# A four-layer graph network in one kernel: when the target rows are turned and exchanged in its first stage, and the order of two products in its second

## The chip, the cores and the metric

The kernel runs on one core of a Trainium2 chip. The metric is the time of one execution on the device, in microseconds (us); lower is better. TensorE is written PE in the rows (PEld: its weight loads), VectorE DVE, ScalarE ACT, GpSimd POOL, and SP is the engine that does nothing here but issue transfers.

## The reference

Four graph layers run one after the other on a table of 100,000 nodes with 128 features each, and 50,000 edges (`src`, `dst`, sorted by `dst`). After each layer the result is added to its input and each row is normalized. Layers 0 and 1 are those of this change:

```python
def _L0_gnn_ref(x, W, b, src, dst):
    diff = x[dst] - x[src]
    max_diff = jax.ops.segment_max(diff, dst, num_segments=x.shape[0])
    max_diff = jnp.where(jnp.isneginf(max_diff), 0, max_diff)
    return jax.nn.relu(jnp.concatenate([x, max_diff], axis=1) @ W + b)

def _L1_gnn_ref(x, feature1, feature2, edge_index, batch, ...):
    src, dst = (edge_index[0], edge_index[1])
    x = _swish(x @ lin_W.T + lin_b)
    f1 = feature1 @ f1_W1.T @ f1_W2.T
    f2 = feature2 @ f2_W1.T @ f2_W2.T
    agg1 = jax.ops.segment_sum(f1 * x[src], dst, num_segments=n)
    h1 = agg1 @ conv1_rel_W.T + conv1_rel_b + x @ conv1_root_W.T
    h1 = _swish(h1 @ lin1_W.T + lin1_b)
    agg2 = jax.ops.segment_sum(f2 * x[src], dst, num_segments=n)
    h2 = ...                                   # as h1, with the second set of weights
    h = jnp.concatenate([h1, h2], axis=1) @ cat_W.T + cat_b
    h = h + x
    for i in range(3):
        h = _swish(h @ lins_W[i].T + lins_b[i]) + h
    ...                                        # graph norm over all nodes, final product

x = _layernorm(x + _L0_gnn_ref(x, L0_gnn_W, L0_gnn_b, src, dst))
x = _layernorm(x + _L1_gnn_ref(x, edge_attr_54, edge_attr_18, edge_index, batch0, ...))
...                                            # layers 2 and 3 in the same manner
```

## The kernel before

Nodes and edges are cut into blocks of 512 rows (4 tiles of 128): 196 node blocks (`NB`) and 98 edge blocks (`EB`). The program is a row of stages with a barrier between them. The change touches two of them:

- **nodes01** computes, for every node block, layer 0 without edges and the part of layer 1 that needs none, and for every edge block the rows of those nodes that have incoming edges in layer 0. Each engine has a hand-written order of work in `step(t)`, one step for each node block, with an edge block in every second step. So an even step and the odd step behind it make a **pair**: two node blocks and one edge block. Engines meet only at semaphores (`wait_ge`).
- **edges1** does layer 1 once more for the nodes that have edges, one edge block a step, with the two segment sums as scans.

In nodes01 an edge block goes this way. POOL gathers the target rows into `p_xd` (L729). DVE turns them in squares of 32 by 32 into `p_xdt` (`turn_squares`, L138). SP exchanges the groups of 32 partitions with four transfers into `p_xdT` (`swap_groups`, L156). PE multiplies them: L817, in the odd step, then L818 for the running minimum `p_run` of the scan (L986). DVE adds and normalizes (L967, L993, L212, L1002), POOL raises to the power -1/2 (L761), DVE makes the shift `p_nm` (L957) and ACT applies both (L227). Node blocks go through the same statistics, and then through h1, h2 (L797, L800, L860, L862), their concatenation (L826, L827, then L973 on DVE) and three residual layers: products L784, L806 and L832 on PE, activations L848 on ACT, additions L903 on DVE. The rest is turned and exchanged in the same way for `p_xT` (input rows) and `p_x1T` (normalized rows); all three exchanges are issued by SP in one hand-written order, behind waits:

```python
for t in range(0, NB + 12, 2):          # SP, nodes01: one turn for each pair
    ...                                 # p_xT, load of x, store of p_o, store of p_oe
    ...                                 # hT, p_x1T, p_xdT, t1T, pen
```

In edges1 the steps of PE end with the concatenation (L1264, L1265), the third residual product (L1270) and the product of the block's own rows (L1275), whose activation `q_xx` (L1334) is what L1228 of the next step multiplies. The residual products are L1222, L1242 and L1270, with L1293 on ACT and L1355 on DVE behind each; L1422 on DVE is behind L1265; L1432 and L1437 are the two scans.

Of the kernel before, what the change touches and what calls it, by code (L numbers as in the profile page):

```python
# [13 lines left out]
G = 4  # L14
# [546 lines left out]
def nodes01(nc, a, tab, s, first, arrivals, ring, to_edges1, NB, EB):  # L561


    with ExitStack() as ctx:
# [65 lines left out]
        def _(sp):  # L630
# [3 lines left out]
            for t in range(0, NB + 12, 2):  # L634
# [16 lines left out]
                if live(e, EB):  # L651
                    sp.wait_ge(e_applied, e + 1)
                    sp.dma_start(e_v[e], oe[:, e % 2]).then_inc(e_saved[e % 2], DMA)
                n = t - 12
# [10 lines left out]
                e = t // 2 - 1 - BEHIND  # L665
                if live(e, EB):
                    sp.wait_ge(xd_squared, e + 1)
                    after(sp, e_product, e - 1)
                    swap_groups(sp, xdT[:, e % 2].rearrange("p j a i -> p a j i"), xd_turned[:, :, :], xdT_in[e % 2])
# [225 lines left out]
        def _(dve):  # L895
# [17 lines left out]
            def step(t):  # L913
# [45 lines left out]
                if even and e.live(EB):  # L959
                    dve.wait_ge(xd_in[e.of(2)], landed(2, e, G))  # L960
                    if e.past(1):
                        dve.wait_ge(xdT_in[e.back(1).of(2)], landed(2, e.back(1), 4))
                    turn_squares(nc, xd_turned[:, :, :].rearrange("p c (j i) -> p c j i", j=G), xd[:, e.of(2)]).then_inc(xd_squared, 1)
# [34 lines left out]
                if not even and q.live(QB):  # L998
                    lo, hi = batch(q)
                    dve.wait_ge(counted, counted_by(q))  # L1000
                    after(dve, rooted, q.b - 1)
                    nc.vector.tensor_scalar(guard[:, q.of(2), lo:hi], st[:, q.of(2), lo:hi, SQUARES], 1.0 / H, LN_EPS,  # L1002
                                            ALU.mult, ALU.add).then_inc(guarded, 1)
            n_chain = [0]
# [58 lines left out]
def edges1(nc, a, tab, s, ring, to_edges1, h_saved, NB, EB, LAST):  # L1063


    with ExitStack() as ctx:
# [148 lines left out]
        def _(pe):  # L1215
            def step(t):
# [43 lines left out]
                if n.live(EB):  # L1260
                    pe.wait_ge(h1_ready, n.b + 1)
                    pe.wait_ge(h2_ready, n.b + 1)
                    after(pe, r0_ready, n.b)
                    nc.tensor.matmul(flat(bank_h), s["cat"][:, 0, :], h1[:, n.of(2), :], start=True, stop=False)  # L1264
                    nc.tensor.matmul(flat(bank_h), s["cat"][:, 1, :], h2[:, n.of(2), :],  # L1265
                                     start=False, stop=True).then_inc(cat_done, 1)
                n = t.back(2)
# [4 lines left out]
                if t.live(EB):  # L1272
                    pe.wait_ge(own_in[t.of(4)], landed(4, t, 4))
                    pe.wait_ge(active_g, t.b + 1)
                    nc.tensor.matmul(flat(bank_l), s["lin"][:, :], by_row(flat(own[:, t.of(4)])),  # L1275
                                     start=True, stop=True).then_inc(lined_o, 1)
# [12 lines left out]
        def _(act):  # L1289
# [10 lines left out]
            def step(t):  # L1300
# [27 lines left out]
                n = t.back(2)  # L1328
                if n.live(EB):
                    residual(2, n)  # L1330
                if t.live(EB):
                    act.wait_ge(lined_o, t.b + 1)
                    after(act, r0_ready, t.b - 1)
                    nc.scalar.activation(xx[:, t.of(2), :], flat(bank_l), ACT.Silu, bias=col(LIN_B)).then_inc(active_o, 1)  # L1334
                if t.fixed and t.b == MASK_AT:
                    act.wait_ge(turned, 1)
                    nc.scalar.activation(mask16[:, 0:4, :], bank_t[0:MC, 0:4, :], ACT.Copy).then_inc(copied, 1)
                    act.wait_ge(turned, 2)
                    nc.scalar.activation(mask16[:, 4:7, :], bank_t[0:MC, 0:3, :], ACT.Copy).then_inc(copied, 1)
# [959 lines left out]
```

## Time and profile before

| | |
|---|---|
| median of 3 runs | 5377.8 us (5353.22, 5377.8, 5377.81) |
| profiled execution, its own time | 5359.57 us |
| its span, first to last instruction | 5357.8 us |
| PE busy | 4172.5 us, 78% of the span |
| DVE busy | 4291.2 us, 80% |
| ACT busy | 3570.0 us, 67% |
| POOL busy | 4022.1 us, 75% |
| nodes01, its first and last turn of target rows | 67.0 and 1857.6 us |
| edges1, roughly | from 1900 to 3000 us |

Busy is the time in which an engine executes something; the rest of the span it waits. PE's ends of matmuls are modelled, so that a matmul of 512 columns reads as 1.02 us for its two passes although the next begins 0.86 us after it did. For the order of events on PE, read starts.

### The profile page before, as it was taken

The page shows a single profiled execution, that of the slowest core. Times are in us where ns is not written, and L with a number is a line of the kernel's source. Part 1 is how long each engine was busy: PE and PEld are TensorE (multiplying, and loading weights), DVE is VectorE, ACT ScalarE, POOL GpSimd, SP SyncE. Part 2 cuts the span into 40 slices and gives each one's busy share as a digit, 9 for nine tenths or more (in the row PEclk, how much of TensorE's full clock was granted, in tenths as well). Part 3 has the DMA queues.
Part 4 walks back from the last instruction along what each step waited for, and adds up shares of the span by engine and source line. Part 5 has one row for each costly group of instructions (what it writes and reads, how often), then busy time and mean ns, then how long its engine had stood idle before and what let it go on. Part 6 is the DMA issues. An engine that isn't in the chain of part 4 may idle for free. (4 is left out here: it accounts for less than half of the span.)

```text
span 5357.8 us, 82513 instructions
## 1 busy us (share of the span) xinstructions
PE 4172.5 (78%) x18043; PEld 2613.2 (49%) x18166; DVE 4291.2 (80%) x8844; ACT 3570.0 (67%) x9029; POOL 4022.1 (75%) x4129
## 2 busy tenths in 40 slices
PE   6899999999999969999999888888577745550000
PEld 3455555555555534444444588878454535540000
DVE  7789888889999748887888799999788844457776
ACT  3667766667777636666666688888688844446665
POOL 6677877778787777777777277777777767777777
PEclk9999999999999989999999999999655557665555
DMA  7888998999999748777777699999799867774443
GB/s 191 199 217 224 220 226 218 219 218 230 226 229 225 182 107 244 204 205 206 208 204 207 227 380 375 376 375 379 262 284 282 278 202 229 230 238 151 136 135 102
DMA packets 1057580, 1239.08 MB, mean 231 GB/s; under 512 B 554591, under 2 KB 724121, under 8 KB 1057335
## 3 DMA queue, kind: packets, MB, share of 16 engines
q1 hardware_dynamic: 951542, 1085.52, 65.5%
q0 software_dynamic: 100352, 149.23, 13.1%
q10 hardware_dynamic: 5440, 1.80, 0.1%
q14 instruction: 182, 1.48, 0.1%
q8 instruction: 64, 1.05, 0.1%
HBM read 648.66 MB, written 438.76 MB: 203 GB/s over the span
## 5 line engine op out<-in xcount | busy, mean ns | idle before, releaser
L848 ACT ACTIVATE p_s<-p_ps,cols 128x512 f32<-128x512 f32 x588 | 402.2, 684 | 192.6 <-PE p_ps L832 119.6
L1199 POOL DMA_INDIRECT ring_rows<-t_rows,home_cols x384 | 419.1, 1091 | 118.9 <-issue 88.3
L198 POOL DMA_INDIRECT out<-u_res,scatter_cols x392 | 406.9, 1038 | 121.8 <-issue 118.1
L191 POOL DMA_INDIRECT u_rows<-t_rows,home_cols x392 | 387.5, 988 | 145.6 <-issue 118.6
L191 POOL DMA_INDIRECT ring_rows<-t_rows,home_cols x400 | 394.7, 987 | 129.6 <-issue 114.3
L736 POOL DMA_INDIRECT home<-edge_row_cols,scatter_cols x392 | 401.8, 1025 | 119.2 <-issue 119.2
L729 POOL DMA_INDIRECT p_xs<-in_x,src_cols x388 | 393.3, 1014 | 123.0 <-issue 114.0
L729 POOL DMA_INDIRECT p_xd<-in_x,dst_cols x388 | 384.6, 991 | 106.8 <-issue 95.7
L1208 POOL DMA_INDIRECT home_cols<-home,src_cols x376 | 378.0, 1005 | 111.4 <-issue 86.0
L227 ACT ACTIVATE p_o<-p_v,p_nm,p_rs 128x128 f32<-128x128 f32 x784 | 321.5, 482 | 138.6 <-DVE p_nm L957 137.6
L212 DVE BATCH_NORM_STATS2 r_counts<-r_v 128x6 f32<-128x256 f32 x980 | 373.2, 422 | 10.6 <-issue 0.5
L227 ACT ACTIVATE r_x<-r_v,r_nm,r_rs 128x128 f32<-128x128 f32 x784 | 321.7, 482 | 82.3 <-DVE r_nm L1779 82.3
L1832 ACT ACTIVATE u_o<-u_x,cols,u_rs 128x128 f32<-128x128 f32 x392 | 161.0, 482 | 286.9 <-DVE u_x L1821 286.9
L1293 ACT ACTIVATE q_s<-q_ps,cols 128x512 f32<-128x512 f32 x294 | 202.0, 687 | 184.6 <-PE q_ps L1270 131.0
L1612 PEld LDWEIGHTS r_ps_n<-r_wn,r_h 128*128 128x128 f32 x2352 | 313.4, 194 | 10.5 <-issue 0.3
L1612 PE MATMUL r_ps_n<-r_wn,r_h 128*128 128x128 f32 x2352 | 313.5, 277 | 5.4 <-issue 0.3
L1590 POOL TENSOR_TENSOR r_v<-r_x,default_row 128x512 f32<-128x512 f32 x192 | 244.3, 1273 | 71.8 <-ACT r_x L227 71.8
L761 POOL TENSOR_TENSOR p_rs<-p_guard,minus_half 128x12 f32<-128x12 f32 (+2 forms) x101 | 236.7, 2344 | 76.7 <-DVE p_guard L1002 76.0
L234 PE MATMUL u_ps_s<-ident,u_weighted 128*128 128x128 f32 x392 | 104.4, 420 | 227.9 <-DVE u_weighted L2190 227.7
L903 DVE TENSOR_TENSOR p_r<-p_s,p_r 128x512 f32<-128x512 f32 x392 | 261.3, 667 | 19.2 <-ACT p_s L848 19.1
L791 PEld LDWEIGHTS p_ps<-w_swapped,p_xT 128*128 128x128 f32 x1568 | 221.2, 202 | 113.1 <-issue 102.3
L860 ACT ACTIVATE p_h<-p_ps,cols 128x512 f32<-128x512 f32 x196 | 134.7, 687 | 211.7 <-PE p_ps L797 211.7
(305 smaller groups left out, 13770.7 us busy)
## 6 DMA issues: line engine op xcount, KB each, us to landing
ring_rows<-in_x SPq DMA_DIRECT2D x98, 512.0 KB, 6.5
p_xT<-p_xt SPq DMA_DIRECT2D x392, 128.0 KB
t_rows<-p_o SPq DMA_DIRECT2D x98, 512.0 KB
p_x1T<-p_oT SPq DMA_DIRECT2D x392, 128.0 KB
hT<-ring_own SPq DMA_DIRECT2D x98, 512.0 KB
q_hn<-hT SPq DMA_DIRECT2D x98, 512.0 KB, 4.7
r_h<-hT SPq DMA_DIRECT2D x98, 512.0 KB
r_x<-t_rows SPq DMA_DIRECT2D x98, 512.0 KB
```

Of the source, the lines that this page charges most:

```text
L191: nc.gpsimd.indirect_dma_start(out=rows[:, j, :], out_offset=None, in_=table, in_offset=bass.IndirectOffsetOnAxis(ap=idx[:, j:j + 1], axis ...
L198: nc.gpsimd.indirect_dma_start(out=table, out_offset=bass.IndirectOffsetOnAxis(ap=idx[:, j:j + 1], axis=0), in_=rows[:, j, :], in_offset=N ...
L212: i = nc.vector.bn_stats(st[:, j:j + 2, :].rearrange("p j k -> p (j k)"), v[:, j:j + 2, :].rearrange("p j f -> p f j"))
L227: i = nc.scalar.activation(dst[:, j, :], v[:, j, :], ACT.Identity, bias=nm[:, j:j + 1], scale=rs[:, j:j + 1])
L729: nc.gpsimd.indirect_dma_start(out=rows[:, j, :], out_offset=None, in_=a["x"], in_offset=bass.IndirectOffsetOnAxis(ap=idx[:, j:j + 1], axi ...
L736: nc.gpsimd.indirect_dma_start(out=tab["home"], out_offset=bass.IndirectOffsetOnAxis(ap=s["scat"][:, k:k + 1], axis=0), in_=s["at"][:, k:k ...
L848: nc.scalar.activation(act_out[i][:, :], flat(bank_r if i else bank_t), ACT.Silu, bias=col(LS0 + i)).then_inc(r_act[i], 1)
L903: nc.vector.tensor_tensor(hs[i + 1][:, n.of(4 if i == 2 else 2), :], act_out[i][:, :], hs[i][:, n.of(2), :], ALU.add).then_inc(r_added[i], 1)
L1199: nc.gpsimd.indirect_dma_start(out=rows[:, e % 4, j, :], out_offset=None, in_=tab["t1"], in_offset=bass.IndirectOffsetOnAxis(ap=s["home"][ ...
L1208: nc.gpsimd.indirect_dma_start(out=s["home"][:, k:k + 1], out_offset=None, in_=tab["home"], in_offset=bass.IndirectOffsetOnAxis(ap=s["src" ...
L1590: nc.gpsimd.tensor_tensor(v3[:, n % 6], x3[:, n % 4], to4(s["default"]), ALU.add).then_inc(summed3, 1)
L1612: i_mm = nc.tensor.matmul(bank_n[i % 2][:, j, :], h[:, i % 6, tile(j)], wn[:, :], start=False, stop=i > 0 and j == G - 1)
```

## The change

In nodes01, DVE turns the target rows at the end of the odd step ahead of the pair that uses them, instead of in the middle of that pair's even step, and SP issues their exchange ahead of the store of hT and of the exchange of `p_x1T`, instead of behind both. In edges1, PE multiplies the block's own rows ahead of the third residual product instead of behind it, and ACT has the two activations in the same new order. No work is added or left out, and no buffer is changed.

```diff
@@ nodes01, SP
                 if live(e, EB):
                     sp.wait_ge(e_applied, e + 1)
                     sp.dma_start(e_v[e], oe[:, e % 2]).then_inc(e_saved[e % 2], DMA)
+                e = t // 2 - 1 - BEHIND
+                if live(e, EB):
+                    sp.wait_ge(xd_squared, e + 1)
+                    after(sp, e_product, e - 1)
+                    swap_groups(sp, xdT[:, e % 2].rearrange("p j a i -> p a j i"), xd_turned[:, :, :], xdT_in[e % 2])
                 n = t - 12
                 if live(n, NB):
                     sp.wait_ge(r_added[2], n + 2)
@@
                     swap_groups(sp, x1T[:, q % 2], o_turned[:, q % 2], x1_in[q % 2])
-                e = t // 2 - 1 - BEHIND
-                if live(e, EB):
-                    sp.wait_ge(xd_squared, e + 1)
-                    after(sp, e_product, e - 1)
-                    swap_groups(sp, xdT[:, e % 2].rearrange("p j a i -> p a j i"), xd_turned[:, :, :], xdT_in[e % 2])
@@ nodes01, DVE, step(t)
-                if even and e.live(EB):
-                    dve.wait_ge(xd_in[e.of(2)], landed(2, e, G))
-                    if e.past(1):
-                        dve.wait_ge(xdT_in[e.back(1).of(2)], landed(2, e.back(1), 4))
-                    turn_squares(nc, xd_turned[:, :, :].rearrange("p c (j i) -> p c j i", j=G), xd[:, e.of(2)]).then_inc(xd_squared, 1)
@@ at the end of step(t), behind the guard
+                n = e.back(-1)
+                if not even and n.live(EB):
+                    dve.wait_ge(xd_in[n.of(2)], landed(2, n, G))
+                    if n.past(1):
+                        dve.wait_ge(xdT_in[e.of(2)], landed(2, e, 4))
+                    turn_squares(nc, xd_turned[:, :, :].rearrange("p c (j i) -> p c j i", j=G), xd[:, n.of(2)]).then_inc(xd_squared, 1)
@@ edges1, PE, step(t)
+                if t.live(EB):
+                    pe.wait_ge(own_in[t.of(4)], landed(4, t, 4))
+                    pe.wait_ge(active_g, t.b + 1)
+                    nc.tensor.matmul(flat(bank_l), s["lin"][:, :], by_row(flat(own[:, t.of(4)])),
+                                     start=True, stop=True).then_inc(lined_o, 1)
                 n = t.back(2)
                 if n.live(EB):
                     pe.wait_ge(r_added[1], n.b + 1)
                     nc.tensor.matmul(flat(bank_r), s["lins"][:, 2, :], hs[2][:, n.of(2), :],
                                      start=True, stop=True).then_inc(r_done[2], 1)
-                if t.live(EB):
-                    ...
@@ edges1, ACT, step(t)
-                n = t.back(2)
-                if n.live(EB):
-                    residual(2, n)
                 if t.live(EB):
                     act.wait_ge(lined_o, t.b + 1)
                     after(act, r0_ready, t.b - 1)
                     nc.scalar.activation(xx[:, t.of(2), :], flat(bank_l), ACT.Silu, bias=col(LIN_B)).then_inc(active_o, 1)
+                n = t.back(2)
+                if n.live(EB):
+                    residual(2, n)
```

On DVE in nodes01, from the guard (L1002) that closes an odd step, before:

```order
 L1002 TENSOR_SCALAR p_guard<-p_st 128x12
 L903 TENSOR_TENSOR ring_own<-p_s,p_r 128x512
 L138 STREAM_TRANSPOSE p_oT<-p_o 128x4x128
 L903 TENSOR_TENSOR p_r<-p_s,p_r 128x512
 L138 STREAM_TRANSPOSE p_xt<-ring_rows 128x512
 L938 TENSOR_TENSOR p_v<-p_ps,b_row 128x512
 L940 SCALAR_TENSOR_TENSOR p_v<-p_v,ring_rows 128x512
 L212 BN_STATS p_st<-p_v 128x6 x2
 L903 TENSOR_TENSOR p_r<-p_s,p_r 128x512
 L957 SCALAR_TENSOR_TENSOR p_nm<-p_st,p_rs 128x12
 L138 STREAM_TRANSPOSE p_xdt<-p_xd 128x512
 L973 SCALAR_TENSOR_TENSOR p_r<-p_ps,cols,p_xx 128x512
```

and in the changed kernel, where the guard is L997 and L973 is L968:

```order
 L997 TENSOR_SCALAR p_guard<-p_st 128x12
 L138 STREAM_TRANSPOSE p_xdt<-p_xd 128x512
 L903 TENSOR_TENSOR ring_own<-p_s,p_r 128x512
 L138 STREAM_TRANSPOSE p_oT<-p_o 128x4x128
 L903 TENSOR_TENSOR p_r<-p_s,p_r 128x512
 L138 STREAM_TRANSPOSE p_xt<-ring_rows 128x512
 L938 TENSOR_TENSOR p_v<-p_ps,b_row 128x512
 L940 SCALAR_TENSOR_TENSOR p_v<-p_v,ring_rows 128x512
 L212 BN_STATS p_st<-p_v 128x6 x2
 L903 TENSOR_TENSOR p_r<-p_s,p_r 128x512
 L957 SCALAR_TENSOR_TENSOR p_nm<-p_st,p_rs 128x12
 L968 SCALAR_TENSOR_TENSOR p_r<-p_ps,cols,p_xx 128x512
```

The turn of `p_xd` has passed nine instructions: it now stands ahead of the three L903 of the even step, and nothing stands between L957 and L968 (L973 before).

On SP in nodes01, one turn of its loop, before:

```order
 L653 DMA t_rows<-p_oe 128x512
 L657 DMA hT<-ring_own 128x1024
 L156 DMA p_x1T<-p_oT 128x1x256 x4
 L156 DMA p_xdT<-p_xdt 128x4x32 x4
 L143 DMA t_edge_squares<-p_oeT 128x512
```

and in the changed kernel:

```order
 L653 DMA t_rows<-p_oe 128x512
 L156 DMA p_xdT<-p_xdt 128x4x32 x4
 L662 DMA hT<-ring_own 128x1024
 L156 DMA p_x1T<-p_oT 128x1x256 x4
 L143 DMA t_edge_squares<-p_oeT 128x512
```

The four transfers into `p_xdT` have passed the store of hT and the four of `p_x1T`.

On PE in edges1, from the end of one step into the next, before:

```order
 L1264 MATMUL q_ps<-q_h,cat 128x512
 L1265 MATMUL q_ps<-q_h,cat 128x512
 L1270 MATMUL q_ps<-q_r,lins 128x512
 L1275 MATMUL q_ps<-ring_rows,lin 128x512
 L1222 MATMUL q_ps<-q_r,lins 128x512
 L1228 MATMUL q_ps<-q_xx,R 128x512
 L1230 MATMUL q_ps<-q_run,A 128x512
```

and in the changed kernel, where every line is one further down:

```order
 L1265 MATMUL q_ps<-q_h,cat 128x512
 L1266 MATMUL q_ps<-q_h,cat 128x512
 L1271 MATMUL q_ps<-ring_rows,lin 128x512
 L1276 MATMUL q_ps<-q_r,lins 128x512
 L1223 MATMUL q_ps<-q_r,lins 128x512
 L1229 MATMUL q_ps<-q_xx,R 128x512
 L1231 MATMUL q_ps<-q_run,A 128x512
```

The own rows' product now has two products, not one, between it and the one that needs its activation.

## Rows read from the trace of the kernel before

**Rows 1.** Busy time by engine in windows of nodes01 and edges1 (us; engines; clock; DMA).

```profile
1300.00:1500.00 200.00, 200.00 (x761) 113.08 (x760) 182.17 (x325) 142.73 (x267) 160.97 (x145) 1.00 0.93 228
...
2200.00:2400.00 200.00, 200.00 (x693) 90.89 (x692) 162.08 (x279) 121.54 (x238) 156.53 (x183) 1.00 0.73 205
```

**Rows 2.** All turns of `p_xd` in the program: count, duration, first and last start.

```profile
L138 DVE STREAM_TRANSPOSE p_xdt<-p_xd x98: 701/705/710, 67.0 to 1857.6; 128x512 f32<-128x512 f32 x98
```

**Rows 3.** Waits in nodes01, 100 to 1850 us: who waited for whom; total, times, longest.

```profile
DVE p_ve L967 <- PE p_ps L818: 65.7, 78, 13.8
...
PE p_ps L817 <- issue: 36.0, 21, 11.6
```

**Rows 4.** Timeline of a pair of nodes01: start, length, engine, line [idle before <- releaser].

```profile
1511.62 0.75 DVE L973 SCALAR_TENSOR_TENSOR p_r<-p_ps,cols,p_xx 128x512 f32<-128x512 f32 x1 [1.03 <-PE p_ps L827]
...
1514.49 0.70 DVE L138 STREAM_TRANSPOSE p_oT<-p_o 128x512 f32<-128x512 f32 x1
...
1515.12 0.65 DVE L903 TENSOR_TENSOR p_r<-p_s,p_r 128x512 f32<-128x512 f32 x1
...
1518.42 0.69 DVE L903 TENSOR_TENSOR p_r<-p_s,p_r 128x512 f32<-128x512 f32 x1
...
1519.11 0.70 DVE L138 STREAM_TRANSPOSE p_xdt<-p_xd 128x512 f32<-128x512 f32 x1
...
1519.66 1.02 PE L832 MATMUL p_ps<-p_r,lins 128*128 128x512 f32 x2
...
1536.94 0.70 DVE L138 STREAM_TRANSPOSE p_xdt<-p_xd 128x512 f32<-128x512 f32 x1
...
1537.49 1.02 PE L832 MATMUL p_ps<-p_r,lins 128*128 128x512 f32 x2
```

**Rows 5.** Timeline of nodes01 where L832 came late, even step.

```profile
1500.58 0.68 DVE L903 TENSOR_TENSOR p_r<-p_s,p_r 128x512 f32<-128x512 f32 x1
...
1501.31 1.12 PE L832 MATMUL p_ps<-p_r,lins 128*128 128x512 f32 x2
...
1502.27 1.02 PE L839 MATMUL p_ps<-p_x1T,lin_swapped 128*128 128x512 f32 x2
```

**Rows 6.** Timeline of nodes01: exchanges of target rows and their products.

```profile
786.55 2.99 SPq L156 DMA_DIRECT2D p_xdT<-p_xdt  x4
...
791.59 1.02 PE L806 MATMUL p_ps<-p_r,lins 128*128 128x512 f32 x2
...
795.11 0.77 PE L817 MATMUL p_ps<-w_sum,p_xdT 128*128 128x128 f32 x2 [2.50 <-issue]
...
1519.84 2.67 SPq L156 DMA_DIRECT2D p_xdT<-p_xdt  x4
```

**Rows 7.** Timeline of SP in nodes01, near 190 us.

```profile
189.91 1.26 SPq L657 DMA_DIRECT2D hT<-ring_own  x1
...
195.68 3.95 SPq L156 DMA_DIRECT2D p_xdT<-p_xdt  x4
```

**Rows 8.** Timeline of a step of edges1.

```profile
2403.46 1.02 PE L1265 MATMUL q_ps<-q_h,cat 128*128 128x512 f32 x2
...
2404.52 0.75 DVE L1422 SCALAR_TENSOR_TENSOR q_r<-q_ps,cols,q_xx 128x512 f32<-128x512 f32 x1 [0.62 <-PE q_ps L1265]
...
2405.18 1.02 PE L1275 MATMUL q_ps<-ring_rows,lin 128*128 128x512 f32 x2
...
2406.24 0.69 ACT L1334 ACTIVATE q_xx<-q_ps,cols 128x512 f32<-128x512 f32 x1 [0.17 <-PE q_ps L1275]
...
2406.98 1.13 PE L1228 MATMUL q_ps<-q_xx,R 128*128 128x512 f32 x2
...
2407.94 1.02 PE L1230 MATMUL q_ps<-q_run,A 128*128 128x512 f32 x2
...
2408.77 0.65 DVE L1355 TENSOR_TENSOR q_r<-q_s,q_r 128x512 f32<-128x512 f32 x1
...
2409.66 1.02 PE L1242 MATMUL q_ps<-q_r,lins 128*128 128x512 f32 x2
```

More of the change, by code:

```diff
@@ L1271, in step @@
                                      start=True, stop=True).then_inc(r_done[2], 1)
-                if t.live(EB):
[L1273 to L1276, printed above, removed]
                 if t.fixed and t.b == MASK_AT:
```

## The prediction

> **What bounds the kernel now.** I read the table of busy time by windows first. In late nodes01 and in edges1 PE reads as busy for all of 200 us, DVE for 182 and 162, ACT for less [rows 1]. PE's ends are modelled, so the starts have to confirm it. They do in the timeline: two turns of target rows in a quiet pair are 17.83 us apart, and so are two L832 [rows 4], with matmuls of 512 columns starting every 0.86 us. PE sets the pace there.
>
> Next I asked how far the whole stage is from that pace. 98 turns start between 67.0 and 1857.6 us [rows 2]: (1857.6 - 67.0) / 97 = 18.46 us a pair, 0.63 us over the quiet one, 61 us over the stage. The list of waits says where part of it is: L817, the product of the target rows, waited 21 times, 36.0 us in total, once for 11.6 us [rows 3]. DVE's L967 behind it shows the same holes. The releaser is given as "issue", so no engine ended the wait. The timeline gives the missing one: SP issued the exchange from 786.55 to 789.54; L806 started at 791.59, so L817 was due at 791.59 + 0.86 = 792.45; it started at 795.11 [rows 6]. The scan that it also needs belongs to DVE and would have been named. The exchange took 5.6 us from its last issue. In the quiet pair it is issued from 1519.84 on and is in time.
>
> In edges1 the timeline shows one wait of PE in each step. L1265 and L1275 start at 2403.46 and 2405.18, two matmuls apart, 0.86 each. L1228 is two further on and due at 2406.90. It starts at 2406.98, just behind the activation of L1275's product (2406.24 + 0.69 = 2406.93), and L1230 follows 0.96 later, not 0.86 [rows 8]. So the step loses 0.08 + 0.10 = 0.18 us.
>
> **The change, part by part.**
>
> *The exchange earlier.* The turn moves from 1519.11 to the place behind the guard, ahead of the L903 in front of the L138 that starts at 1514.49 [rows 4], about 1513.9: 5.2 us earlier. SP has by then stored `p_oe` and waits for hT. The longest wait other than the one of 11.6 is under 3 us in the timeline that I read, so 5 us cover it. The gather is long done (POOL works on it in the first half of the same pair), and the exchange of the block before was needed by L817 in this step already: the new waits cost nothing. hT and `p_x1T` go out 2.7 us later, the length of four issues [rows 6]. `p_x1T` is used a full pair later, and DVE's buffers turn over in two pairs: nothing. Gain: 36.0 - 11.6 = 24.4 us. To it belongs what follows a wait: in the row of 795.11 two passes take 0.77 us, so the clock was lower behind it, and the L832 of the next even step is late too [rows 5, 6]. This lies between 0 and the rest of the excess, 61 - 36 = 25 us; much of that is extra DVE work in the first pairs. I take 7.
>
> *The wait of 11.6 us.* SP was busy with one-time transfers until 185 and reached this exchange at 195.68; in the new order it stands where hT stood, 189.91 [rows 7]: 5.8 us gained.
>
> *The price on DVE.* Before, the turn filled a hole: it ended at 1519.81, and L973 behind it had to wait for L827 anyway. In its new place it stands in an unbroken run. From L973 of the odd step (1511.62, which itself had waited for PE's L827) to the L903 that ends at 1519.11 DVE works without a gap [rows 4]. That L903 releases L832. How late may it be? Where L832 waited, L903 ended at 1501.26, L832 started at 1501.31, and L839 came 0.96 instead of 0.86 behind: 0.05 + 0.10 = 0.15 us from DVE's end to an effective start [rows 5]. In the quiet pair L903 ended 0.55 us ahead of L832 (1519.11, 1519.66): room of 0.40. The turn costs the run one spacing of a transpose, 1515.12 - 1514.49 = 0.63 us [rows 4]. So L832 is late by 0.63 - 0.40 = 0.23 us in each even step: 97 x 0.23 = 22.3 us lost. What is queued behind L832 on PE all shifts with it; ACT's L227 starts 0.63 later as well, but has about that much room before the next product needs ACT. Bounds: nothing, if DVE's run has slack that I don't see; 0.63 a pair, 61 us, if all room is used up elsewhere. The row nearest is L903 against L832, so I take 0.23.
>
> *edges1.* L1275 moves up by one matmul, 0.86 us, and its wait of 0.18 has to vanish. What is late next? L1242 needs L1355. DVE runs without a break from L1422 (released by L1265, 2404.52) to the end of L1355, 2409.42; plus the 0.15 of above gives 2409.57, and L1242 started at 2409.66 [rows 5, 8]. This chain hangs on L1265, not on L1228, so it doesn't get shorter: only about 0.07 to 0.09 of the 0.18 can be had. 98 steps less some ten at the start: 88 x 0.07 = 6.2 us. Bounds 0 and 88 x 0.18 = 15.8. The third residual's activation comes 0.86 later, still ahead of the second scan's end: hidden.
>
> *Sum.* 24.4 + 7 + 5.8 - 22.3 + 6.2 = 21.1 us gained. The profiled execution took 5359.6 us (span 5357.8 and 1.8 around it), so 5338.5 against that. The three runs shown are 5353.2, 5377.8 and 5377.8; with the profiled one the mean is 5367.1. They differ by 24.6 us, more than the gain, and lateness of transfers is a likely part of that. I carry the sum to the mean: 5367.1 - 21.1 = 5346. The median shown is 10.7 above that mean, so against it the same sum looks like 0.6%.
>
> **A page weighed.** L817 started 2.66 us after it was due, 5.6 us after the last issue of its exchange had ended [rows 6]. The Trainium skill, page "SBUF — State Buffer", section "The DMA setup-cost knee", gives every transfer about 2 us that don't depend on its bytes. By that rule the exchange would have been there at about 791.6, L817 would never wait, and moving the exchange would be worth nothing. The trace disagrees in 21 of 98 pairs. Of the time it would make the last rival below, by its rows 5383 us.
>
> **Rivals.**
> - *No price on DVE and all of edges1* (0.15). L832 keeps its room, and L1242's wait shrinks with the rest: 24.4 + 7 + 5.8 + 15.8 = 53 us, 5314. For it: DVE is busy for only 182 of 200 us. Against: the 18 us idle are at L967 and L973, behind the run.
> - *The run on DVE costs more than it brings* (0.13), the one on the other side. The same L903 is held by more than the turn, for instance by `p_nm` and ACT's L227 that now come 0.63 later and push L848 and L891. At the full 0.63 a pair: 43.4 - 61 = 18 us lost, 5385. It decides from 0.45 us a pair on (43.4 / 97); slower by over 0.5% needs 0.73.
> - *The exchange isn't what is late* (0.12). If L817 waits for something else, or the exchange is no sooner there for being issued sooner, the terms of the exchange fall away and the price and edges1 remain: -22.3 + 6.2 = 16 us lost, 5383. For it: the list of waits names nobody. Against: the scan ends long before, and long issues and long waits stand together [rows 6].
> - *The forecast* (0.60).
>
> **How the numbers follow.** 0.5% is about what a measurement of this kernel can tell from no change: 27 us, so 5351 against the median. The forecast is 5346 with its own range of 5330 to 5362, on both sides of 5351: 0.33 faster, 0.27 same. First rival: all faster. Second: 0.07 same, 0.06 slower. Third: 0.11 same, 0.01 slower. Faster 0.48, same 0.45, slower 0.07. The range leaves out the far part of the first rival and the far part of the second and third: 5318 to 5378.
>
> **What the profile after would show.** L817 without waits but the one near 190 us, there about 6 us shorter. PE's L832 in each even step ended by DVE's L903, and two turns of target rows about 18.06 us apart instead of 17.83, the same in all pairs. DVE's L968 (L973 before) idle for 0.6 us in the even step. In edges1, L1229 (L1228 before) without a wait for ACT; L1243 (L1242) released by DVE, steps 0.07 us shorter. The prediction is wrong if quiet pairs stay at 17.83, if they grow beyond 18.3, or if L817 still waits.

## The result, and the profile after

| | median us | runs |
|---|---|---|
| before | 5375.8 | 5353.2, 5373.8, 5377.8, 5377.8 |
| changed | 5340.3 | 5339.0, 5339.4, 5341.3, 5344.5 |

The ratio is 0.9945, with an interval of 0.9918 to 0.9972: faster by 0.55%, and by at least 0.28%, at 5340 where 5346 was forecast. One execution in this whole document, of `e8_turn_twice` below, fell in a slower state (7974.8 us) and stands in no median or ratio. The profiled execution took 5339.03 us (span 5337.3) against 5359.6: 20.6 us, where the sum said 21.1. The steps have to be checked one by one, since a right sum can hide two wrong terms.

First the windows of [rows 1] in the changed kernel, with the same columns (PE, PEld, DVE, ACT, POOL busy; clock; DMA share; GB/s). PE is still busy for all but 0.2 us of each, at full clock; DVE's 181 and 162 us are about those of before (182 and 162).

```profile
1300.00:1500.00 200.00, 199.83 (x754) 111.17 (x753) 181.22 (x322) 139.15 (x266) 159.86 (x144) 1.00 0.88 226
2200.00:2400.00 200.00, 200.00 (x709) 91.85 (x707) 161.94 (x279) 122.59 (x239) 156.14 (x186) 1.00 0.74 208
```

The waits of nodes01 from 100 to 1850 us, as in [rows 3] (who for whom; total, times, longest):

```profile
DVE p_r L968 <- PE p_ps L827: 100.9, 100, 1.3
...
PEld p_ps L832 <- DVE p_r L903: 72.9, 95, 0.9
...
DVE p_ve L962 <- PE p_ps L818: 44.3, 94, 9.1
...
PE p_ps L817 <- issue: 7.1, 1, 7.1
```

L817's 21 waits have become one, 36.0 us have become 7.1. The price stands two rows above it: PE's weight load for L832 now waits for DVE's L903 for 72.9 us in 95 waits, where the list of before has about half of that:

```profile
PEld p_ps L832 <- DVE p_r L903: 34.4, 94, 0.8
```

DVE's row behind L818 fell from 65.7 to 44.3 with the holes that it mirrored.

The turns over the whole program, which answer to [rows 2]:

```profile
L138 DVE STREAM_TRANSPOSE p_xdt<-p_xd x98: 704/709/712, 62.1 to 1831.1; 128x512 f32<-128x512 f32 x98
```

From first to last they take 1769.0 us, 18.24 a pair, instead of 18.46. A quiet pair, against [rows 4, 5]:

```profile
1495.30 1.12 PE L832 MATMUL p_ps<-p_r,lins 128*128 128x512 f32 x2
...
1507.47 0.71 DVE L138 STREAM_TRANSPOSE p_xdt<-p_xd 128x512 f32<-128x512 f32 x1
1508.10 0.65 DVE L903 TENSOR_TENSOR ring_own<-p_s,p_r 128x512 f32<-128x512 f32 x1
...
1512.38 1.02 PE L827 MATMUL p_ps<-p_h,cat 128*128 128x512 f32 x2
...
1512.59 0.67 DVE L903 TENSOR_TENSOR p_r<-p_s,p_r 128x512 f32<-128x512 f32 x1
...
1513.31 1.12 PE L832 MATMUL p_ps<-p_r,lins 128*128 128x512 f32 x2
1513.44 0.75 DVE L968 SCALAR_TENSOR_TENSOR p_r<-p_ps,cols,p_xx 128x512 f32<-128x512 f32 x1
1514.27 1.02 PE L839 MATMUL p_ps<-p_x1T,lin_swapped 128*128 128x512 f32 x2
```

This is the price itself. L903 ends at 1513.26, L832 starts 0.05 later, and L839 comes 0.96 behind it, not 0.86. L827 started 0.93 ahead of L832, so L832 lost 0.07 in starting and 0.10 behind, 0.17 in all. Two L832 are 18.01 apart here. Quiet pairs repeat in fours. By the starts of L817 they take 18.10, 18.00, 18.00 and 18.15 us in this trace, 18.07 in the mean; where no exchange was late, before has 17.83 three times and then 18.05, 17.89 in the mean. Like for like the price is 0.18 us a pair: the 17.83 of the prediction is the most frequent pair of before, not the mean one. The order also reads plainly: the turn stands ahead of the L903 that writes `ring_own`, and that one and six more rows of DVE lie between it and the L903 that releases L832.

SyncE's queue, near 190 us (answers to [rows 7]) and in the quiet pair (answers to [rows 6]); the one wait left is PE's row:

```profile
190.14 4.24 SPq L156 DMA_DIRECT2D p_xdT<-p_xdt  x4
194.42 2.93 SPq L662 DMA_DIRECT2D hT<-ring_own  x1
...
199.22 0.77 PE L817 MATMUL p_ps<-w_sum,p_xdT 128*128 128x128 f32 x2 [7.10 <-issue]
...
1508.20 2.64 SPq L156 DMA_DIRECT2D p_xdT<-p_xdt  x4
1510.90 1.51 SPq L662 DMA_DIRECT2D hT<-ring_own  x1
1512.52 2.90 SPq L156 DMA_DIRECT2D p_x1T<-p_oT  x4
```

The exchange is issued 0.02 us behind the turn, and its last issue ends at 1510.84, 8.65 us before L817 starts. That is also the median over all exchanges, with 4.84 the least (the one that L817 waited for); before has 3.2 and 2.5. It also has hT and `p_x1T`, 512 KB each, behind it in the queue now and not ahead of it. Which of the two matters is a question for the experiments.

A step of edges1, as in [rows 8]:

```profile
2401.89 1.02 PE L1271 MATMUL q_ps<-ring_rows,lin 128*128 128x512 f32 x2
2402.09 0.75 DVE L1423 SCALAR_TENSOR_TENSOR q_r<-q_ps,cols,q_xx 128x512 f32<-128x512 f32 x1 [0.62 <-PE q_ps L1266]
...
2402.95 0.69 ACT L1332 ACTIVATE q_xx<-q_ps,cols 128x512 f32<-128x512 f32 x1 [1.34 <-PE q_ps L1271]
...
2404.46 1.02 PE L1229 MATMUL q_ps<-q_xx,R 128*128 128x512 f32 x2
...
2405.32 1.02 PE L1231 MATMUL q_ps<-q_run,A 128*128 128x512 f32 x2
...
2406.34 0.65 DVE L1356 TENSOR_TENSOR q_r<-q_s,q_r 128x512 f32<-128x512 f32 x1
...
2407.04 1.13 PE L1243 MATMUL q_ps<-q_r,lins 128*128 128x512 f32 x2
```

L1229 has its operand 0.82 us early (2402.95 + 0.69 = 2403.64, start 2404.46) and L1231 follows 0.86 behind it: that wait is gone. L1243 now starts 0.05 us behind the end of DVE's L1356: it is the late one, as forecast.

Where the 20.6 us lie, by the end of the last instruction of each stage in the two traces: nodes01 ends 21.9 us sooner (1884.6, 1862.7), edges1 takes 4.9 less (1131.0, 1126.2), nodes23 2.5 less, and the rest 8.7 more (1546.5, 1555.2). That rest has nothing of the change in it; over all traces of this study it takes 1546 to 1569 us with no relation to the kernel, and the trace of before had the shortest. So 20.6 against a sum of 21.1 is partly luck: nodes01 gave 7.0 us more than its four terms (24.4 + 7 + 5.8 - 22.3 = 14.9), and stages that the change doesn't touch took 6.2 back.

### The profile page after: what moved, and what is told of

The parts are those of the page before. It is cut to its first block and busy times, and to the rows that moved or that the text cites. A ratio compares the mean times of both kernels' runs of the same rounds, so it can differ in the third digit from the quotient of the medians.

```text
span 5337.3 us, 82636 instructions
## 1 busy us (share of the span) xinstructions
PE 4178.1 (78%) x18166; PEld 2602.5 (49%) x18166; DVE 4292.4 (80%) x8844; ACT 3557.6 (67%) x9029; POOL 4019.2 (75%) x4129
## 5 line engine op out<-in xcount | busy, mean ns | idle before, releaser
L729 POOL DMA_INDIRECT p_xd<-in_x,dst_cols x388 | 396.0, 1021 | 107.5 <-issue 101.4
L903 DVE TENSOR_TENSOR p_r<-p_s,p_r 128x512 f32<-128x512 f32 x392 | 261.6, 667 | 18.3 <-ACT p_s L848 17.7
L2191 DVE TENSOR_TENSOR u_weighted<-u_rows,edge_weight_cols 128x512 f32<-128x512 f32 x98 | 67.5, 689 | 255.3 <-DMA u_rows<-t_rows,home_cols 255.3
```

What stands on the lines that cost most here:

```text
L729: nc.gpsimd.indirect_dma_start(out=rows[:, j, :], out_offset=None, in_=a["x"], in_offset=bass.IndirectOffsetOnAxis(ap=idx[:, j:j + 1], axi ...
L903: nc.vector.tensor_tensor(hs[i + 1][:, n.of(4 if i == 2 else 2), :], act_out[i][:, :], hs[i][:, n.of(2), :], ALU.add).then_inc(r_added[i], 1)
```

## The experiments

Before was timed anew beside each set of kernels: 5401.9 us beside the first four, 5369.4 beside the next four, 5370.3 beside the last four. Ratios are to that.

### Each half alone

`e1_nodes01_only` has the change without its part in edges1 (the turn in DVE's stream, the exchange in SyncE's), `e2_edges1_only` has that part alone.

> The part in nodes01 alone: turn and exchange moved, edges1 as before. My theory (late exchanges removed, L832 held by DVE for 0.23 us in each even step): nodes01 ends about 22 us earlier than in the profile of before, pairs of 18.07 us, edges1 steps stay at 10.92 us; span about 22 us under that of before. Rival (the gain comes from edges1 or from chance differences in later stages): nodes01 shorter by less than 10 us.

> The part in edges1 alone: own rows' product and activation ahead of the third residual's, nodes01 as before. My theory (the wait of L1228 goes, and L1242 takes most of its place): steps of 10.84 to 10.87 us instead of 10.92, the stage 5 us shorter, the time 5 us under before, which a measurement hardly tells; L817 in nodes01 waits again some 30 to 50 us in total, differently from run to run. Rival (all 0.18 us of a step come back): 10.74 us a step, 16 us.

`e1_nodes01_only` took 5343.7 us, ratio 0.9899 (0.9875 to 0.9923): 58 us faster than a before that was itself slow there. In its trace, of the slowest of its six executions (5357.7 us), nodes01 ends at 1862.8, 21.8 us sooner than in that of before, as expected. The span is only 1.8 us shorter, where 22 were expected, since edges1 and the untouched stages from edges2 on took 4 and 23 us more, and nodes23 7 less. `e2_edges1_only` took 5397.8, ratio 1.001 (0.9992 to 1.0029). Its trace has edges1 4.5 us shorter than that of before, which is less than its runs differ (5385 to 5430), and it says why before was slow beside it: its nodes01 is that of before, L817 waited 63.5 us up to 1880 us of the span, and nodes01 ends at 1920.6, 36.0 us later than in the trace of before.

### The two parts of the exchange's move

`e3_turn_alone` moves only DVE's turn, `e4_queue_alone` only SyncE's exchange:

```diff
 # e4_queue_alone, SyncE in nodes01; DVE as before
+                e = t // 2 - 1 - BEHIND
+                if live(e, EB):
+                    sp.wait_ge(xd_squared, e + 1)
+                    after(sp, e_product, e - 1)
+                    swap_groups(sp, xdT..., xd_turned..., xdT_in[e % 2])
                 (hT is stored)
-                (the same five lines, behind hT and p_x1T)
```

> DVE turns the target rows at the odd step's end, but SP issues their exchange where it did before, behind the store of hT and the exchange of p_x1T; edges1 as before. The exchange then is issued about 1.3 us earlier than before (SP gets to it at about 1518.6 on the clock of the profile, not 1519.8). Theory that the price sits on DVE and the gain in the issue time: L832 is held by L903 in all even steps (quiet pairs 18.07 us, 22 us lost), and of the 29 us of L817's waits only about half go: the time within 10 us of before, and above e1_nodes01_only by 10 to 20 us. Rival (the gain comes from the place of the turn on DVE, not from SP): as fast as e1_nodes01_only.

> SP's order changed alone, turn on DVE where it was; edges1 as before. SP waits for the turn (about 1519.8) ahead of hT and p_x1T, so the exchange of target rows is issued no earlier than before in a quiet pair, and hT and p_x1T 5 to 7 us later. Theory: quiet pairs stay at 17.83 us, L832 isn't held, L817 waits as often as before except near 190 us, where it waits about 5 us less: 0 to 8 us faster than before. Rival (it is the place in SP's queue that counts, not the time of issue): L817's waits go, 30 us or more faster than before.

| | median us | ratio | quiet pair, mean of four | L817 waited |
|---|---|---|---|---|
| `e2_edges1_only` (nodes01 as before) | 5397.8 | 1.001 (0.9992 to 1.0029) | 17.89 | 63.5 |
| `e3_turn_alone` | 5392.6 | 0.9973 (0.9953 to 0.9993) | 18.07 | 35.9 |
| `e4_queue_alone` | 5358.6 | 0.9927 (0.9903 to 0.9952) | 17.89 | 44.1 |
| `e1_nodes01_only` | 5343.7 | 0.9899 (0.9875 to 0.9923) | 18.07 | 6.7 |

The lists of waits up to 1880 us, of `e2_edges1_only`:

```profile
PE p_ps L817 <- issue: 63.5, 40, 10.2
```

and of `e4_queue_alone`, in the execution of 5379.5 us, the slowest of its five:

```profile
PE p_ps L817 <- issue: 44.1, 29, 11.8
```

`e3_turn_alone` went in part as expected: the price is paid in each pair, the waits are 28 us less, and 9 us are gained. But it is 49 us above `e1_nodes01_only`, where 10 to 20 were expected. `e4_queue_alone` was a miss. My theory gave it 0 to 8 us, since the exchange is issued no sooner: in the traces of before and of this kernel the first issue follows the end of the turn by less than 0.1 us in 96 and 97 of 98 pairs. By the medians it gained 43, and its five executions (5354.6 to 5379.5) lie nearly all below the 24 of before (5378.0 to 5429.9).

What differs is what is in the queue ahead of the exchange's four issues: in before 1 MB of hT and `p_x1T`, here nothing of that. It would be easy to say that those bytes held the exchange up, but the trace doesn't bear it out. This is one of its late exchanges, with hT and `p_x1T` issued behind it:

```profile
637.63 2.67 SPq L156 DMA_DIRECT2D p_xdT<-p_xdt  x4
...
642.67 1.02 PE L806 MATMUL p_ps<-p_r,lins 128*128 128x512 f32 x2
...
645.64 0.46 PE L817 MATMUL p_ps<-w_sum,p_xdT 128*128 128x128 f32 x2 [1.95 <-issue]
```

L817 was due at 642.67 + 0.86 = 643.53 and started 5.34 us after the last issue ended (640.30). Where L817 waited for more than 0.3 us in this trace, it started 3.0 to 5.4 us after the last issue, 4.5 in the mean; in before that was 3.1 to 5.6 us, 4.3 in the mean. So an exchange with nothing of hT and `p_x1T` ahead of it takes as long as one behind them (whether the same bytes right behind it hold it up is not tested), and the 44.1 us of waits lie between the 36.0 and 63.5 of the two traces that have the old order. Where the 43 us of the medians come from is therefore open: the one trace is of the slowest execution. What the traces do show is what made the waits go. With the queue's order alone 29 are left, with the turn alone 18 (the last issue then ends 4.4 us ahead of L817 in the median, and not 3.2), and with both, at 8.65 us, one.

### The turn in the idle time of the odd step

DVE idles in the odd step ahead of L968, for L827. `e5_turn_in_hole` is the changed kernel with the turn there:

```diff
 # DVE, nodes01: behind L962 of the odd step, not behind the guard
+                if not even and n.live(EB):
+                    ... turn_squares(nc, xd_turned..., xd[:, n.of(2)]).then_inc(xd_squared, 1)
                 (L968, L988, statistics, L997 guard)
-                if not even and n.live(EB):
-                    ... (the same)
```

> The changed kernel once more, beside the next three. Where its time is 5339 to 5345 us on a chip on which the kernel before takes 20 to 60 us more, the gain over before is not a fixed number: it is what L817's waits happen to cost there.

> The changed kernel with the turn of target rows once more moved: into the odd step, between L967 and L973 of before, where DVE waits 1.03 us for PE. Theory (the price is the 0.63 us in DVE's unbroken run, of which 0.40 were room): quiet pairs back at 17.83 us, L832 not held, L817 without waits: 22 us faster than the changed kernel, about 5318. Rival (pairs of 18.07 us are what PE or POOL now need, or the gathers are too late for a turn at that place): as fast as the changed kernel or slower.

`changed_again` took 5339.5 us, ratio 0.9952 (0.9933 to 0.9972); `e5_turn_in_hole` 5321.7, ratio 0.992 (0.9897 to 0.9942): 18 us less than the changed kernel. Its timeline:

```profile
1493.61 1.02 PE L832 MATMUL p_ps<-p_r,lins 128*128 128x512 f32 x2
...
1509.93 0.69 DVE L962 TENSOR_TENSOR p_ve<-p_ps,b_row 128x512 f32<-128x512 f32 x1 [0.25 <-PE p_ps L818]
1510.53 0.70 DVE L138 STREAM_TRANSPOSE p_xdt<-p_xd 128x512 f32<-128x512 f32 x1
1511.45 1.02 PE L832 MATMUL p_ps<-p_r,lins 128*128 128x512 f32 x2
```

Two L832 are 17.84 apart again, and a group of four pairs takes 17.90 in the mean (17.83 three times, then 18.10). So the same transpose costs 0.18 us a pair behind the guard and 0.01 here, one wait of DVE further up. nodes01 ends 12.4 us sooner than in `changed_again` (1847.9, 1860.3).

### The turn twice

`e8_turn_twice` has a second transpose of the same rows into a scratch tile directly ahead of the turn.

> The changed kernel with a second transpose of the same size (128x512, into a scratch tile) directly ahead of the turn in nodes01: the same term of the price, doubled. Theory: DVE's run from the second gate to the last residual's sum has no room left, so all of the 0.63 us lands on each pair: quiet pairs of 18.70 us where the changed kernel has 18.07, L832 of the even step held by DVE's L903 in every pair, and 97 x 0.63 = 61 us more than the changed kernel, about 5401. Rival: a part of the 0.63 is still taken up by idle time behind the turn, then the pairs come to 18.2 to 18.5 and the time to 5355 to 5385. Leaves nothing of the computation out.

```profile
1492.76 0.71 DVE L138 STREAM_TRANSPOSE p_spare<-p_xd 128x512 f32<-128x512 f32 x1
1493.39 0.67 DVE L138 STREAM_TRANSPOSE p_xdt<-p_xd 128x512 f32<-128x512 f32 x1
1499.20 1.13 PE L833 MATMUL p_ps<-p_r,lins 128*128 128x512 f32 x2
...
1517.91 1.13 PE L833 MATMUL p_ps<-p_r,lins 128*128 128x512 f32 x2
```

L833 is L832 of the others: 18.71 apart. The quiet pairs take 18.60 to 18.71, 18.66 in the mean, and the median of its five executions is 5397.8, ratio 1.0054 (1.0029 to 1.008), 58 us above `changed_again`, which ran on another chip. The first transpose costs 0.18 us a pair, the second 0.59 of its 0.63: the room is all but used up by the first, as the prediction's sum had it, and it was about 0.45 (0.63 - 0.18), not 0.40.

### edges1: the turn behind the first residual, and a miss

L1243 waits for L1356, and DVE's turn stands right ahead of that. `e6_edges1_turn_later` puts it behind; `e7_both` has this and the hole of nodes01.

```diff
 # DVE, edges1
-                e = t.back(-TURN_AHEAD)
-                if e.past(4) and e.live(EB):
-                    turn(e)
                 n = t.back(2)
                 if n.live(EB):
                     residual(0, n)
+                e = t.back(-TURN_AHEAD)
+                if e.past(4) and e.live(EB):
+                    turn(e)
```

> The changed kernel with one more edit, in edges1: DVE turns the gathered rows behind the first residual's addition (L1356 of the changed kernel, which L1243 waits for), not ahead of it. Theory (L1243 is held by DVE's run from L1266 on): the run is 0.63 us shorter, L1243 isn't held, steps of 10.73 us and not 10.87: 10 to 12 us faster than the changed kernel. Rival (something else holds the step at 10.84 to 10.87, POOL's gathers with 10.9 us of work in a step for instance): no difference.

> Both of the edits before together. By my theory they add up: 32 to 34 us faster than the changed kernel, about 5307. By the rivals 0 to 12.

Both missed: 5380.0 us, ratio 1.0016 (0.9986 to 1.0045), and 5367.5, ratio 1.0001 (0.9979 to 1.0024). In the trace of the first kernel 50 of 97 steps do take 10.73 us, but the mean of steps 10 to 90 is 11.5, where the changed kernel has 10.92. The list of waits from 1900 to 3030 us has this row, where the changed kernel has 13.9 us in 2 waits:

```profile
DVE q_squares L138 <- DMA ring_rows<-t_rows,home_cols: 246.3, 88, 7.5
```

and the timeline where that happens:

```profile
2691.10 1.25 DVE L1438 TENSOR_TENSOR_SCAN q_run<-ring_cont,q_run,q_m 128x512 f32<-128x512 bf16 x1
2691.27 1.85 POOL L1209 DMA_INDIRECT home_cols<-home,src_cols  x1 [0.27 <-POOL q_idle L1186]
...
2692.27 0.66 DVE L1356 TENSOR_TENSOR ring_own<-q_s,q_r 128x512 f32<-128x512 f32 x1
...
2692.86 0.68 DVE L1356 TENSOR_TENSOR q_r<-q_s,q_r 128x512 f32<-128x512 f32 x1
2693.43 0.96 POOL L1209 DMA_INDIRECT home_cols<-home,src_cols  x1 [0.30 <-issue]
...
2695.03 0.71 DVE L138 STREAM_TRANSPOSE q_squares<-ring_rows 128x512 f32<-128x512 f32 x1 [1.49 <-DMA ring_rows<-t_rows,home_cols]
...
2699.14 0.69 DVE L1415 TENSOR_TENSOR q_m<-q_ps,q_xs 128x512 f32<-128x512 f32 x1 [0.99 <-PE q_ps L1257]
2699.30 0.96 POOL L1200 DMA_INDIRECT ring_rows<-t_rows,home_cols  x1 [0.30 <-issue]
```

GpSimd is never idle for longer than its 0.3 us between instructions, in this kernel or in the changed one. Its groups by line, from 2100 to 2800 us (count | busy, mean ns | idle before), first in the changed kernel:

```profile
L1200 POOL DMA_INDIRECT ring_rows<-t_rows,home_cols x257 | 282.3, 1098 | 76.1 <-issue 58.5 <-POOL q_idle L1186 17.6
L1209 POOL DMA_INDIRECT home_cols<-home,src_cols x257 | 250.4, 974 | 76.1 <-issue 58.8 <-POOL q_idle L1186 17.3
```

then in `e6_edges1_turn_later`:

```profile
L1200 POOL DMA_INDIRECT ring_rows<-t_rows,home_cols x243 | 274.1, 1128 | 72.2 <-issue 55.9 <-POOL q_idle L1186 16.3
L1209 POOL DMA_INDIRECT home_cols<-home,src_cols x243 | 268.1, 1103 | 72.0 <-issue 55.5 <-POOL q_idle L1186 16.5
```

A step has four of each: 257 / 4 = 64.25 steps in 700 us are 10.9 a step, 243 / 4 = 60.75 are 11.5, the measured steps in both cases. An undisturbed gather takes 0.958 us (mean of the 129 of that window beside which DVE has no instruction with both inputs in SBUF). With that a step would cost GpSimd an estimated 8 x 0.958 + (76.1 + 76.1 + 15.8) / 64.25 = 10.28 us (15.8 is its memsets). So for steps of 10.73 it has 0.45 us for being held up, and the gathers are held up for 8 x (1.036 - 0.958) = 0.62 us in the changed kernel and 8 x (1.115 - 0.958) = 1.26 here.

### Is it GpSimd?

`e9_seven_gathers` is `e6_edges1_turn_later` with one gather of eight taken from GpSimd, `e10_changed_seven` the changed kernel with the same, and `e11_both_ahead2` is `e7_both` with the turn two steps ahead of its use and not three, which gives each gather one step more. The first two leave a quarter of the gathered target rows out and copy others, so they don't compute the reference; they only measure what a gather less is worth:

```diff
 # e9, e10: GpSimd
                     for j in range(G):
-                        nc.gpsimd.indirect_dma_start(out=rows[:, e % 4, j, :], ...)
+                        if j < G - 1 or e < 4:
+                            nc.gpsimd.indirect_dma_start(out=rows[:, e % 4, j, :], ...)
 # e9, e10: SyncE
+                e = t + 4
+                if live(e, EB):
+                    if e >= 5:
+                        sp.wait_ge(squared, e - 3)
+                    sp.dma_start(rows[:, e % 4, G - 1, :], tab["t1"][e * P:(e + 1) * P, :])...
 # e11
-        TURN_AHEAD = 3
+        TURN_AHEAD = 2
                 (the turns ahead of the loop stay as they were)
```

> The kernel with DVE's turn of edges1 behind the first residual (its mean step was 11.52 us, and DVE waited 56 times, 151 us in all, for gathered rows), with GpSimd relieved: from block 4 on the fourth of the eight gathers of a step that fetches target rows is left out, and SyncE copies 128 plain rows of the same table in its place, so a quarter of the rows of those blocks are others than the reference's. Theory (GpSimd's eight gathers set the pace: 8 x 1.26 us and what they are held up while VectorE reads two inputs from SBUF): with 1.26 us less a step GpSimd keeps up, DVE no longer waits for rows, the steps go to 10.73 us, edges1 to about 1115 us from 1172, the time to about 5325. Rival (the late place of the turn itself, or a transfer behind it, is what costs): the steps stay at 11 us or more and the time at 5360 to 5380.

> The control: the changed kernel, turn of edges1 in its old place, with the same seven gathers and the plain copy of SyncE (a quarter of the target rows of blocks from 4 on are others than the reference's). Theory: GpSimd bounds nothing there, the step of 10.87 us is DVE's run from L1423 to L1356 that holds L1243; so the steps stay at 10.85 to 10.87 and the time within 10 us of the changed kernel's. Rival (GpSimd's eight gathers are what sets 10.87): the steps shorten to 10.73 or below here too, 12 us or more faster.

> The kernel with both turns moved (nodes01's into the idle time of the odd step, edges1's behind the first residual; its time was that of before, as edges1 lost what nodes01 won), with edges1's turn two steps ahead of its use instead of three, so that the gathers have one step (10.8 us) more to arrive. If the gathers are only late by a constant, this lets the steps go to 10.73 us with no wait of DVE for rows: edges1 about 1115 us and the time about 5307. If GpSimd cannot deliver eight gathers in 10.73 us, because its gathers are held up by VectorE's instructions, the waits only start a few steps later: steps of 11.3 to 11.6 us again and a time of 5355 to 5375. I hold the second for likelier. Computes what the reference does.

| | median us | ratio | mean of steps 10 to 90 | DVE waited for rows |
|---|---|---|---|---|
| `e9_seven_gathers` | 5313.4 | 0.9893 (0.9869 to 0.9918) | 10.75 | 15.7 us, 3 times |
| `e10_changed_seven` | 5331.4 | 0.9923 (0.9903 to 0.9944) | 10.90 | 11.2 us, 2 times |
| `e11_both_ahead2` | 5323.9 | 0.9889 (0.9849 to 0.993) | 11.09 | 78.7 us, 39 times |

With seven gathers the steps go to 10.73 and stay there (86 of 97), and edges1 takes 1103 us and not 1172. GpSimd has time left, and it shows: in `e9_seven_gathers` it waits for ACT, 79.7 us in the same window.

```profile
L1216 POOL DMA_INDIRECT home_cols<-home,src_cols x260 | 256.0, 985 | 151.3 <-ACT q_s L1301 79.7 <-issue 68.3 <-POOL q_idle L1192 3.3
```

The control moved 8 us, with steps of 10.84 instead of 10.87 in the median: the changed kernel isn't held by GpSimd, though it stands close to it. A gather less also takes a transfer from GpSimd's queue, and this pair of runs doesn't part the two. `e11_both_ahead2` came out between my two cases. One step more leaves 79 us of waits of 245, so lateness is a part; but they don't vanish, and the steps stay at 11.09, so the other part is rate. It is no faster than `e5_turn_in_hole`, 5323.9 and 5321.7 with runs from 5288 to 5329 and from 5312 to 5337. Of the versions that compute all of the reference these two are the fastest, 16 and 18 us below `changed_again`.

## Why the prediction was right, step by step

- **PE sets the pace; L817's waits are the exchange's.** Right. Both windows read the same after, and the waits go with the exchange and with nothing else: 36.0 to 7.1 us, and 63.5 to 6.7 from `e2_edges1_only` to `e1_nodes01_only`. The two terms said 24.4 + 5.8 = 30.2, the trace 28.9. The long one kept 7.1 us, where 5.8 was to be left: issuing took 4.24 us there and not 3.95, and L817 started 4.84 us behind the last issue and not 3.26.
- **What follows a wait, 7 us: too small.** The 97 pairs of L817 take 23.3 us less (1789.5, 1766.2). Of that the waits are 28.9 less and the price is 97 x 0.18 = 17.5 more, so 11.9 came from what had followed the waits: for instance, PE's granted clock in before was 0.50 from 795 to 797, behind the wait at 795.11, and 0.68 in the next 2 us. The bounds were 0 and 25; I had put most of the excess down to extra DVE work of the first pairs. The late L832 of [rows 5] doesn't belong here: L817 waited nowhere from 1210 to 1840 us.
- **The price, 0.23 us a pair.** Right in kind, a little too large: measured 0.18, 17.5 us instead of 22.3. Its model (some room, then all of the 0.63) was tested at three points: 0.01 in the hole, 0.18 behind the guard, 0.18 + 0.59 with a second transpose. Pairs of 18.07 look like a hit of the forecast 18.06, but that was 0.23 over the most frequent pair of before, and the mean quiet pair of before is 17.89.
- **The exchange sooner: right, with one effect that it had not.** The prediction lets the move pay by issuing the exchange 5 us sooner. That is what ends the waits: issued 8.65 us ahead of L817 instead of 3.2, one wait is left, and with either half of the move 18 or 29 are. hT and `p_x1T` going out later cost nothing that shows. But by the same reasoning `e4_queue_alone` was to gain 0 to 8 us, and its medians gained 43. No term of the sum has that, and it stays open.
- **edges1, 6.2 us.** 4.9 by the stage's ends, 0.05 to 0.09 us a step; L1243 took over as the late one, by DVE's run, as the text had it.
- **Signs that failed.** The pairs were to be the same throughout, and vary between 18.00 and 18.15. L968 was to idle for 0.6 in the even step. It doesn't. It starts 1.06 us behind L827 in both kernels (1513.44 behind 1512.38), but the 0.63 us that the turn left free are filled from the front, since L903 and L957 now come that much later in the run. My own price said so; the sign contradicted it.
- **The page weighed.** By the rule of the Trainium skill, page "SBUF — State Buffer", section "The DMA setup-cost knee", about 2 us for a transfer whatever its bytes, the exchange would have been in time and its move worth nothing. The part in nodes01 alone was worth 58 us by the medians: the measurement decides. Where L817 waited in before it started 3.1 to 5.6 us after the last issue ended.
- **The rivals.** No price on DVE: fell with 95 waits of L832. Higher price: fell at 0.18 against 0.45. Exchange not late: fell with the waits.
- **The carry to the median.** The profiled execution gained 20.6 us, the medians 35.5. Before's executions differ by how long L817 waits: two traces with its nodes01 have 36.0 and 63.5 us of waits, and nodes01 ends 36 us apart. The changed kernel has hardly any of that left: its medians were 5340.3 and 5339.5 while before's were 5375.8, 5369.4, 5370.3 and 5401.9. So the gain depends on how much before happens to wait: 30 and 36 us for the change, 58 for its nodes01 part on the chip where before was slowest. The forecast took 21.1 from a mean of 5367.1; that it came within 6 us of the measured median owes something to luck.

## What to carry to other kernels

A small transfer that something waits for is issued as early as its data allow, and the engine that makes the data ready moves with it: each half of the move left more than half of the waiting, both together left one wait. Don't take a gain in the median for a proof of the mechanism: the queue's order alone brought 43 us here, and its trace shows exchanges as late as before. When work moves on a busy engine, look for the last idle time ahead of it that another engine ends, and put it there: behind that point the same 0.63 us transpose cost 0.18 us a pair, in front of it 0.01. Before a stage is made faster, work out the floor of each engine that feeds it: GpSimd had an estimated 10.28 us of work for steps of 10.73, and what looked like 11 us to gain became 40 lost.

## What the runs showed of the hardware

Gathers issued by GpSimd take 0.95 to 0.97 us when undisturbed and up to 2.1 in edges1, and how long goes with what DVE does at the time. In the timeline above the gather that takes 1.85 lies beside the scan L1438 and two L1356, all with inputs in SBUF alone; the one that takes 0.96 lies beside L1415, which has one input in PSUM. From 2100 to 2800 us 172 gathers of the changed kernel and 140 of `e6_edges1_turn_later` take over 1.0 us, and each of them overlaps a DVE instruction with two inputs in SBUF; the 129 and 155 that overlap none take 0.970 us at most. The Trainium skill, page "SBUF — State Buffer", section "Who interferes with whom", says that a VectorE instruction with two SBUF inputs and a GpSimd instruction that reads SBUF contend, for a read interface that they share. These rows agree, and not every overlap costs time: 212 and 191 gathers run beside such an instruction in 1.0 us or less. That GpSimd's gathers are what stops the faster edges1 is shown by `e9_seven_gathers`; that DVE's instructions are what stretches them is read from these overlaps and wasn't tested by itself.

The second thing is how long an exchange of four transfers of 64 KB takes to be usable: where L817 waited for it, it started 3.0 to 5.6 us after the last issue had ended in before and in `e4_queue_alone`, with the core's DMA engines about 0.9 busy in nodes01, and with 1 MB issued ahead of it as well as without. Two kernels that issue it at the same time behind the same turn differ by 43 us in the median; why is not shown.
